# A dense expert's fourth tile moved behind the routed experts, in a four-layer transformer kernel on one core

## The reference, cut to what matters

```python
logits = xf @ w_g                              # N = 2048 tokens, 8 experts
topv, topi = jax.lax.top_k(logits, 2)
probs = softmax over the two chosen
capacity = int(TOP_K * CAP_FACTOR * N / N_EXP) # 640
mask = one_hot(topi of the first choices, then of the second)
rank = cumsum(mask) - 1                        # second choices are counted behind all the first
mask = mask * (rank < capacity)
exp_batches = einsum('nec,nd->ecd', sec_mask, xf)
h = gelu(einsum('ecd,edh->ech', exp_batches, c_fc))       # 128 -> 512
exp_out = einsum('ech,ehd->ecd', h, c_proj)               # 512 -> 128
out = einsum('nec,ecd->nd', cb, exp_out)                  # weighted, then added to x
```

## Time and profile before

| | |
|---|---|
| median of 3 runs | 605.69 us (604.83 to 606.33) |
| profiled execution, time | 607.79 us |
| profiled execution, span of the core | 606.0 us |
| busy: PE, PEld, DVE, ACT, POOL | 85%, 68%, 53%, 40%, 40% |
| mean granted clock of TensorE | 0.885 |
| stretch from the last count of PE to the first routed product | 294.15 to 355.08 us |
| routed experts, to the last result | 355.08 to 421.82 us |
| fillers behind them | 421.65 to 430.34 us |

### The profile page before, as it was taken

How to read it: one execution, slowest core, us unless ns; L and a number is a source line. 1 busy time by engine, 2 the same in 40 slices (tenths; PEclk the granted TensorE clock), 3 DMA queues, 4 the chain that set the end, 5 groups by cost and what they waited for, 6 DMA issues and landing times.

```text
span 606.0 us, 9289 instructions
## 1 busy us (share of the span) xinstructions
PE 514.5 (85%) x3342; PEld 412.7 (68%) x3342; DVE 323.7 (53%) x1125; ACT 240.2 (40%) x477; POOL 242.8 (40%) x354
## 2 busy tenths in 40 slices
PE   3798992798779968979356979998989999999997
PEld 3557592687655636867344969997653688799997
DVE  4867239734887625697420155653475865433334
ACT  3653834132345533345312234431155277244430
POOL 5762957253343013576773034565391160000000
PEclk9799896579659999975677999997999899999999
DMA  8999801110930187200112012110800000000002
GB/s 286 329 167 190 283 6 35 40 39 27 333 103 0 35 208 221 60 0 15 44 54 69 2 44 72 56 42 17 275 7 1 0 2 2 1 0 1 1 2 70
DMA packets 55822, 47.54 MB, mean 78 GB/s; under 512 B 6058, under 2 KB 46200, under 8 KB 55648
## 3 DMA queue, kind: packets, MB, share of 16 engines
q1 hardware_dynamic: 52688, 41.54, 25.0%
q0 software_dynamic: 2656, 4.88, 2.6%
q10 hardware_dynamic: 432, 0.52, 0.3%
HBM read 34.69 MB, written 12.82 MB: 78 GB/s over the span
## 4 chain that ended last, share of the span: by engine, by line
PE 66%; DVE 21%; issue 4%; DMA 2%; ACT 2%; another core or an unknown queue 2%; POOL 2%; ACTq 0%; DVEq 0%; POOLq 0%; SPq 0%
PE ps L1236 9%; PE ps L1172 6%; PE ps L1061 5%; PE ps L1062 4%; PE ps L1063 4%; DVE st L1610 4%; PE ps L701 3%; PE ps L1087 3%; PE ps L814 3%; PE ps L744 2%; PE ps L1057 2%; PE ps L754 2%; PE ps L837 2%; PE ps L817 2%
## 5 line engine op out<-in xcount | busy, mean ns | idle before, releaser
L2035 DVE SCALAR_TENSOR_TENSOR x<-ps,gate,x 128x128 f32<-128x128 f32 x128 | 36.0, 345 | 54.8 <-PE ps L1236 54.8
L1236 PEld LDWEIGHTS ps<-moe_w,big 128*128 128x128 f32 x512 | 61.1, 192 | 3.9 <-issue 1.7
L1236 PE MATMUL ps<-moe_w,big 128*128 128x128 f32 x512 | 61.4, 275 | 0.9 <-DVE x L2024 0.9
L2371 POOL DMA_INDIRECT res<-qT,dest x43 | 42.5, 988 | 48.0 <-DVE qT L2010 40.4
L1498 ACT ACTIVATE big<-ps,col 128x512 f32<-128x512 f32 x64 | 42.2, 689 | 48.2 <-PE ps L1063 48.1
L701 PE MATMUL ps<-con,xn 128*128 128x128 f32 x148 | 29.9, 338 | 27.1 <-ACT xn L1438 15.3
L701 PEld LDWEIGHTS ps<-con,xn 128*128 128x128 f32 x148 | 21.2, 174 | 37.4 <-DVE xn L1628 33.5
L1172 PE MATMUL ps<-moe_w,big 128*128 128x128 f32 x344 | 43.8, 285 | 2.6 <-DVE qT L2010 2.0
L1172 PEld LDWEIGHTS ps<-moe_w,big 128*128 128x128 f32 x344 | 42.0, 200 | 3.5 <-issue 2.2
L1350 ACT ACTIVATE xT<-ps 128x512 f32<-128x512 f32 x41 | 24.1, 589 | 50.8 <-PE ps L701 49.5
L1490 ACT ACTIVATE big<-ps 128x320 f32<-128x320 f32 x56 | 23.2, 439 | 48.7 <-PE ps L1063 42.5
(11 more groups left out here) (345 smaller groups left out, 1231.8 us busy)
## 6 DMA issues: line engine op xcount, KB each, us to landing
ring<-in_ew SPq DMA_DIRECT2D x20, 256.0 KB, 5.2
moe_w<-in_m0w SPq DMA_DIRECT2D x16, 256.0 KB, 6.1
moe_w<-in_m2w SPq DMA_DIRECT2D x16, 256.0 KB, 5.7
tok<-zero SPq DMA_DIRECT2D x1, 2580.0 KB, 28.5
big<-tok SPq DMA_DIRECT2D x7, 322.5 KB, 2.9
res<-zero SPq DMA_DIRECT2D x1, 2048.0 KB, 29.1
moe_w<-in_ew SPq DMA_DIRECT2D x8, 256.0 KB, 5.8
big<-res SPq DMA_DIRECT2D x4, 512.0 KB, 5.4
```

Of the source, the lines that this page charges most:

```text
L1236: last = mm(ps[7 - i % 2 if i >= B else 6 + i % 2][:, cols(c)], big[:, FC * (e % 2) + f, i % B, cols(c)], w[:, e, F + P * f:F + P * f + P] ...
L2035: last = v.scalar_tensor_tensor(out=x[:, C * t + c, :], in0=bank[:, cols(c)], scalar=gate[:, C * t + c, e:e + 1], in1=x[:, C * t + c, :], ...
L2371: g_.indirect_dma_start(out=res_d[name], out_offset=bass.IndirectOffsetOnAxis(ap=dest[:, at:at + 1], axis=0), in_=ysb[:, i % 2, cols(b)], ...
```

## The change

The fourth tile of the dense expert (tile B - 1) is taken out of the loop. PE, ACT and DVE each handle it behind the last routed expert, and the fillers that stood there go from 40 to 8. Its low part is still made with those of the other tiles and is kept in its buffer, so the four diagonals that used this space move to `xT`. Its four chunks of x are added in one piece at the end, and the seven routed experts carry 12 chunks instead of 16. SP issues the weights of the last layer only when the results of the fourth tile have been computed.

The second part: `count_second` writes `ps[1]` instead of `ps[2]`, PE waits for the places of the second choices behind the dense expert instead of ahead of it, and DVE makes the low parts of tiles 0 and 1 ahead of its wait for the counts.

```diff
-BUSY_RETURN = 40
+BUSY_RETURN = 8
-        units0 = {"m0": 0, "whole": 4 * E, "m2": 4 * E + C * B}
-        done0 = {"m0": 0, "whole": E, "m2": E + B}
+        units0 = {"m0": 0, "whole": 4 * E, "m2": 4 * E + C * (B - 1)}
+        done0 = {"m0": 0, "whole": E, "m2": E + B - 1}
+        done0["last"] = done0["m2"] + PLACED["m2"]["n"] * PLACED["m2"]["nb"]
-            return kr_w[:, S + P * (j - 24):S + P * (j - 23)] if j < 28 else rz[:, P * (j - 28):P * (j - 27)]
+            return xT[:, B - 1, P * (j - 24):P * (j - 23)] if j < 28 else rz[:, P * (j - 28):P * (j - 27)]
             placed_traffic("m2", 1)
+            sp.wait_ge(gy_mm, done0["last"] + 1)
             moe_load(sp, "m3", w3, 256, ld_m3)
 # PE
-                    mm(ps[2][:, 0:(nb + 1) * E], ones[:, :], bc(oh[:, c, :], [P, nb + 1, E], [1]), start=c == 0, stop=False)
+                    mm(ps[1][:, 0:(nb + 1) * E], ones[:, :], bc(oh[:, c, :], [P, nb + 1, E], [1]), start=c == 0, stop=False)
-            def whole_expert(loaded):
+            def whole_expert(loaded, late=False):
                 def results(t, units):
                     pe.wait_ge(h_act, units)
-                    if t >= 2:
+                    if t == B - 1:
+                        pe.wait_ge(gy_sb, done0["last"] - 1)
+                    elif t >= 2:
                         pe.wait_ge(gy_sb, done0["whole"] + t - 1)
+                if late:
+                    results(B - 1, hidden(B - 1))
+                    return
                 units = hidden(0)
-                for t in range(B):
-                    nxt = hidden(t + 1) if t + 1 < B else None
+                for t in range(B - 1):
+                    nxt = hidden(t + 1) if t + 2 < B else None
                     results(t, units)
                     units = nxt
                 if name == "m2":
                     pe.wait_ge(idx_ready, 2 * B)
+                    pe.wait_ge(x_high, 1)
                     count_second()
-                    pe.wait_ge(idx_ready, 2 * B + 1)
                 if name == "m2":
                     whole_expert(loaded)
+                    pe.wait_ge(idx_ready, 2 * B + 1)
             placed("m2", 1, ld_m2, None, ["L3"])
+            whole_expert(ld_m2, True)
             keep_busy(ps[2], BUSY_RETURN)
 # ACT
-            def whole_expert(fn):
-                for t in range(B):
-                    if t >= 2:
+            def whole_expert(fn, tiles):
+                for t in tiles:
+                    if t == B - 1:
+                        act.wait_ge(gy_mm, done0["last"] - PLACED["m2"]["nb"])
+                    elif t >= 2:
                         act.wait_ge(gy_mm, done0["whole"] + t - 1)
-            whole_expert(ACT.Gelu)
+            whole_expert(ACT.Gelu, range(B - 1))
             placed("m2", 1, ACT.Gelu, None)
+            whole_expert(ACT.Gelu, (B - 1,))
 # DVE
-                        for c in range(nb * i_ // a["n"], nb * (i_ + 1) // a["n"]):
+                        for c in range((nb - C) * i_ // a["n"], (nb - C) * (i_ + 1) // a["n"]):
             link(v.tensor_tensor(lg2[:, :, :], oh[:, 0:nb, :], oh[:, nb:2 * nb, :], ALU.add))
+            whole_low_of(0)
+            whole_low_of(1)
             dve.wait_ge(gate_ep, 1)
             dve.wait_ge(cum_mm, 2 * B + 1)
-            v.tensor_copy(first_n[:, :], ps[2][:, 0:E])
-            places(ps[2][:, E:(nb + 1) * E].rearrange("p (c e) -> p c e", e=E), slice(nb, 2 * nb), CAP2, "base2")
-            whole_low_of(0)
-            whole_low_of(1)
+            v.tensor_copy(first_n[:, :], ps[1][:, 0:E])
+            places(ps[1][:, E:(nb + 1) * E].rearrange("p (c e) -> p c e", e=E), slice(nb, 2 * nb), CAP2, "base2")
-            for t in range(1, B):
+            for t in range(1, B - 1):
                 whole_out(t)
             prepared("L3")
             evacuate("m2", 1)
+            whole_out(B - 1)
+            dve.wait_ge(gy_sb, done0["last"] + 1)
+            for c in range(nb - C, nb):
+                i = v.scalar_tensor_tensor(out=x[:, c, :], in0=whole_y[:, c, :], scalar=have[:, c:c + 1], in1=x[:, c, :],
+                                           op0=ALU.mult, op1=ALU.add)
+            link(i)
```

More of the change, by code:

```diff
@@ L1044, in count_second @@
                 for c in range(nb):
-                    mm(ps[2][:, 0:(nb + 1) * E], ones[:, :], bc(oh[:, c, :], [P, nb + 1, E], [1]), start=c == 0, stop=False)
+                    mm(ps[1][:, 0:(nb + 1) * E], ones[:, :], bc(oh[:, c, :], [P, nb + 1, E], [1]), start=c == 0, stop=False)
                 pe.wait_ge(oh_ready, 2 * B + 1)
-                o = ps[2][:, E:(nb + 1) * E]
+                o = ps[1][:, E:(nb + 1) * E]
                 mm(o, tri[:, :], oh[:, nb:2 * nb, :].rearrange("p a b -> p (a b)"), start=False, stop=False)
@@ L1956, in whole_out @@
             def whole_out(t):
-                dve.wait_ge(gy_mm, done0["whole"] + t + 1)
+                dve.wait_ge(gy_mm, done0["last"] + 1 if t == B - 1 else done0["whole"] + t + 1)
                 v.tensor_copy(whole_y[:, chunks(t), :], ps[6 + t % 2][:, :].rearrange("p (c d) -> p c d", c=C)).then_inc(gy_sb, 1)
```

## The result

The changed kernel took 598.31 us (597.18 to 599.52) against 604.74 us (600.10 to 606.61) for the kernel before in the same comparison, eight runs each: ratio 0.990, 95% interval 0.986 to 0.993. It is faster by about 6.4 us. The profiled execution of after took 597.18 us with a span of 595.4 us; that of before took 607.79 with a span of 606.0. The spans of that pair differ by 10.6 us, since the profiled execution of before took longer than all eight of these runs; the forecast was 8.5 us less than before.

The account below looks back on a forecast made before the run. PE was taken to bound the kernel (66% of the span), its completions seen late during POOL's long send rows. -6.44 - 2.3 + 0.3 = -8.5 us took the 605.69 us median to 597.2 us, range 592.0 to 601.5.

Parts of the forecast that it names:

- First part, -6.44: Ahead of the routed experts: moving the fourth tile removes 2.87 us of products and 3.57 us of results from gapless PE work.
- the hold: Around the dense expert: matmul completions become visible late during long unbroken POOL sends, clear 1 to 4 us after the row.
- Second part, -2.3: Dense expert: products start up to 9.1 us earlier; half of the third tile's 4.64 us is saved, bounds 0 and 9.1.
- ten units be done at 329.4: Dense expert: with products issued from 294.4 us, ten units instead of eight are through at 329.4 us.
- 3.8 us a unit: Dense expert: units three to eight reach ACT between 306.44 and 329.38 us, a pace POOL limits.
- DVE's copy of the counts is still at 301.3.: Sign of being right, ahead of the dense expert: DVE still copies the second counts at 301.3 us.
- The slower rival: Second counts: early products delay their signal and POOL's second sends, +9 us, 614.8 us; delay should stay under 3; chance 0.06.
- The routed experts move forward as a block.: Routed experts: they start earlier and keep their length; four fewer DVE additions cost nothing, since PE sets the pace.
- Behind the experts, +0.3: Behind the routed experts: the fourth tile and eight fillers take 8.97 us against 8.69 for 40 fillers.
- The rival in which the hold catches the fourth tile: Behind the routed experts: POOL's last five sends delay its units, PE 3.9 us late, net -4.8, 600.9 us; chance 0.13.
- Rows of five sends showed no hold: Argument against the fourth tile being caught: between the earlier experts, rows of five POOL sends delayed no completions.
- What the rival said of the clock (1.8 us): Behind the routed experts: after a wait of 2 to 4 us the clock falls, the results take about 1.8 us more.

Follow-up runs that it names:

- the first part alone: Kernel before with only the fourth tile moved behind the routed experts and 8 fillers: 584.25 us (1.004) in the first group, later 602.60 us (0.994).
- the kernel without the nine fillers: Changed kernel without the nine fillers between PE's wait for the sends and the first transposes ahead of the routed experts: 599.47 us, 0.994 to the kernel before.
- kernel with two or three breaks: Changed kernel, POOL waiting for its sends to land before the 9th and 17th, or also the 25th: 593.80 and 595.87 us, both 0.984 to before.
- the four-send breaks: Changed kernel, POOL waiting after every fourth indirect send until all have landed, in the first group: 595.38 us, 1.024 to the kernel before.
- the second part alone: Kernel before with only early low parts, counts in `ps[1]` and the later wait for places: 581.76 us (0.999) in the first group, later 601.69 us (0.998).

## Why the prediction was right, and where not

The time was right, 597.2 forecast and 598.3 measured, and the reason named (the fourth tile leaves a stretch in which PE has no gap, and is hidden behind the experts) is right where completions are held. That the number came so close is in part luck: the front gained more than forecast, and two losses that are not in the sum took it back. Step by step:

- **First part, -6.44.** Right in front. Before, 347.94 - 329.80 = 18.1 us of gapless work stood between the end of the hold and L1008; after it is 335.92 - 329.19 = 6.7. Of the difference of 11.4 us, 6.44 is the fourth tile. Alone the part gave 8.5 us in front (65.2 to 56.7), of which 1.9 and about 4 were lost again later (columns B to C and C to D); by the times it was 3.5 us faster.
- **Second part, -2.3.** Mis-sized in front. The prediction let ten units be done at 329.4 and saved half of the third tile's products. In the trace ACT had eight GELUs done by 313.2 and none more until 329.27, yet PE had issued all 12 products of the third tile meanwhile: the 4.64 us of the earlier trace rows went whole, and the term in front is 11.4 - 6.44 = 5.0. (The work resumes 40.0 us behind A in both profiles, so nothing was won there.) The step that failed is "3.8 us a unit". That pace is that of one profile; in this one eight units had gone through by 313.2, in and behind a break, and four waited for the end of the row. Alone, the part took 3.4 us off A to B and 1.4 us off the time, and the interval of the latter (0.2 to 2.6) holds the 2.3.
- **"DVE's copy of the counts is still at 301.3."** Wrong: 304.27, 306.89 and 306.50 in three profiles of after; POOL ran dry for 2.1 us. The sends end 37.4 us behind A instead of 36.1. What that cost was not tested; as PE resumes 40.0 us behind A with and without it, it cannot have been much. The slower rival's bound (under 3 us, as POOL pauses without places) held for the first of these; its cause did not, since the first part alone had the count later still (309.02) with no early products.
- **"The routed experts move forward as a block."** Not quite. From A to B the three profiles of after gain 11 to 12 us, and from B to C they lose 1.8 to 3.2 against the second profile of before. Of that, 1.3 us in the first of them are the clock in the first expert: the first part of the change removes gapless work ahead of it. Below, what follows the first 12 routed products on PE, in the changed kernel and then in the kernel before, and the table by time of both (busy times, granted clock, DMA):

```profile
346.21 0.96 PE L1137 MATMUL ps<-con,big 128*128 128x128 f32 x5
```
```profile
356.97 0.71 PE L1129 MATMUL ps<-con,big 128*128 128x128 f32 x5
```
```profile
344.00:348.00 4.00, 4.00 (x22) 3.96 (x21) 0.76 (x2) 2.10 (x5) 0.00 (x0) 0.66 0.28 85
```
```profile
356.00:360.00 4.00, 3.45 (x25) 3.17 (x23) 2.18 (x6) 3.34 (x8) 0.00 (x0) 1.00 0.28 81
```

  The 12 products took 346.21 - 343.05 = 3.16 us, before 356.97 - 355.08 = 1.89. The clock 0.66 is a mix of the two levels, 1.2 and 2.4 GHz. In the three held profiles that keep four tiles in front the 12 products take 1.88 or 1.89 us, in the seven with the tile moved 2.68 to 3.37, though PE waits 2.37 or 2.38 us for DVE ahead of them in before and, but for the kernel without the nine fillers (3.65), in those seven alike; what differs is the work before that wait. The Trainium skill, TensorE: Matmul & The Clock Gate, Loop structure matters more than you think, says that long waits between matmuls let the clock fall; the prediction held this against the tail only, and the rows show a fall at the start as well. The pair of profiles hides this loss, because before had a slow stretch of its own near the end (its last 40 result matmuls took 6.45 us, those of after 4.70): there B to the end of the experts differs by 0.4 us only.
- **Behind the experts, +0.3.** Exactly so in the profile (11.17 against 10.85), with a gap of 0.69 us ahead of the results. But this was the good case. The rival in which the hold catches the fourth tile was given 0.13, priced at 3.6 us more, and came in five of seven profiles at 3.6 to 4.2 (wait and result matmuls against 0.69 and 3.84 us). "Rows of five sends showed no hold" was itself borne out; what failed is that the last row would be one of five. It had eight in those five profiles, and eight in the second profile of the kernel before as well, which the prediction did not have. What the rival said of the clock (1.8 us) came at 1.4 to 1.6.
- **The sum.** -0.7 ahead of A, where the change does nothing, -11.4 from A to B, +0.4 in the routed experts, +0.3 behind them and about +0.7 further on (the wait of 0.80 for the second returned rows) make the 10.6 of this pair. The median moved by 6.4: what the front won above the forecast, the first expert's clock and the caught tile took back, as far as the profiles tell. So the total was right through errors of either sign.

One reading of the prediction needs a correction. It has completions visible late until the row of sends has ended. In the trace of before the count is seen at 301.34 and units at 306.44 and 315.34, while POOL's row goes unbroken from 289.84 to 325.93: the hold delays, and it does not stop everything.

What stays open: what the hold is, and why it is there in one group of runs and not in another. Ends of matmuls in the profile are modelled; the runs do not tell whether the matmul, its write or its signal is late, nor whether PE got its instructions in time, which would also account for its idle time within one tile's results. Neither was tested. No kernel with two or three breaks ran where nothing is held; by the four-send breaks the sends there would end some 2 us later for each break.

## What to carry to other kernels

When an engine's wait is released as "remote" long after the work it waits for, look at what another queue was doing at the moment of release, and test that by a break in that queue: here two waits of 2 us on POOL gave another 5.5 to 6 us, about as much as the whole change. Work moved off a stretch that is held looks cheap and gains only while the hold is there; find out first what sets the end without it (here the sends: PE waited 6.0 and 9.1 us for them). And look at several profiles before a tail is called hidden: 0.7 and 2.7 us of the same wait belonged to the same kernel.

## What the runs showed of the hardware

- In unbroken rows of indirect sends of POOL (0.97 us each, 0.30 apart) completions of PE reached DVE and ACT late: in the first profile of after by 10 to 11 us (the count: modelled end 293.61, seen at 304.27; the results of tile 0: 316.19, seen at 326.37), in the second part alone the count by 4.4 us (296.08, seen at 300.50). Some came through within a row; breaks of 2.1 us or more let all that was waiting through in every profile that had them. Behind such a break completions came on time for 6 to 8 us.
- The same kernel took 582.5 us where this did not occur, and 603 to 606 where it did, 3.5 to 4% more. The rows of sends of the two kernels traced without it are as unbroken and as long.
- PE was caught as well: within the held stretch of after only 21 result matmuls were issued between the third tile's products and 329.19, some of them singly, with "issue" waits of 0.20 to 1.81 us ahead of them, though the program has no wait between them.
- Behind the experts the fourth tile was caught in rows of eight sends (five profiles of five) and not in rows of five (two of two).
- Issues of SP's DMAs took 1.06 and 1.28 us where they stood beside the fourth tile's work on DVE (417.95 and 419.06), most of the others 0.43 to 0.47; the four loads took 2.07 us instead of 1.74. What slowed them was not tested.
